# Masking the segment maxima of a graph attention kernel behind their transposition, with a mask that already lies in SBUF

## The chip, the cores and the metric

The kernel runs on one core of a Trainium2 chip. The metric is the device time of one execution in microseconds (us), taken as the median over several executions.

## What is computed

A graph attention layer with a feed-forward block is followed by a top-2 mixture of experts over 6250 nodes of 256 features. 100,000 edges, sorted by destination, carry attention of 8 heads. The part that matters here, cut from the reference:

```python
e = jax.nn.leaky_relu(a_src[src] + a_dst[dst], NEG_SLOPE)
emax = jax.ops.segment_max(e, dst, num_segments=N)
ee = jnp.exp(e - emax[dst])
denom = jax.ops.segment_sum(ee, dst, num_segments=N)
alpha = ee / denom[dst]
msg = h[src] * alpha[:, :, None]
agg = jax.ops.segment_sum(msg, dst, num_segments=N)
```

## The kernel before, in words

The program has four stages one behind another: nodes, edges, the layer's feed-forward block, experts. The change lies in the edge stage. It goes through the edges in 55 groups of 8 steps. A step is a block of 256 edges seen from one window of 128 destination nodes. 16 indirect gathers on GpSimd fetch the source rows of a group (L762), up to four groups ahead.

Every engine runs a loop written by hand over g = -1 to 55, which works in one turn on three groups: n = g + 1 (its maxima), g (its scores and messages) and g - 1 (its sums). The engines run their own instructions in the order in which they are written and meet through counting semaphores. In one turn, from the scan of group n on:

1. VectorE scans a_src along the edges with segment restarts (`tensor_tensor_scan`, L1053), so that the last edge of each segment holds the segment's maximum. It then multiplies by a row mask that is 1 at those last edges (L1055). The mask is `seg_last`, [64, 256], which SyncE loads per group from the scratch tensor `step_last` (L797).
2. TensorE turns the result, [64, 256] to [128, 2 x 64], into `b_cand` (L925).
3. ScalarE and VectorE split the values into three bf16 parts: high part (L876, ScalarE), rest (L1075, VectorE), middle part (L886, ScalarE), low part (L1080, VectorE). 16 products with one-hot matrices (L937, TensorE) then pick each node's maximum. VectorE reads that at the start of the next turn (L967).
4. In between VectorE computes the scores of group g (L1061, L1067, L1069, L1071). ScalarE takes the exponential (L883) and VectorE multiplies the gathered rows by it: `messages(g, 0)` to `messages(g, 2)`, three instructions on L1016. Four small ones (also L1016) follow in the next turn.
5. Behind L886 ScalarE widens the one-hot matrices of group g to f32 (L891, semaphore `oh_wide`). Without them TensorE cannot start the sums of group g.
6. Behind L937 TensorE does the sums of group g: eight steps of L948 for k = 0 to 7, two f32 matmuls a step, with a product for the residual (L828, L829) between k = 1 and k = 2 in 49 of the 55 turns. A f32 matmul has two records in the trace, so a step has four. VectorE adds each step's sum to its window (L1042), in the order of k.

The same mask lies in SBUF in another layout as well, `last_col`, [128, steps, 2], made once in the node stage. ScalarE copies its columns into the candidates (L873).

Of the kernel before, what the change touches and what calls it, by code (L numbers as in the profile page):

```python
# [10 lines left out]
ALU = mybir.AluOpType  # L11
# [3 lines left out]
P = 128  # L15
# [5 lines left out]
def build(nc, x, src, dst, gW, att_src, att_dst, g_bias, gW_res, ln1_g, ln1_b, ln2_g, ln2_b,  # L21
          f_w1, f_b1, f_w2, f_b2, Wr, br, ln_g, ln_b, W1, b1, W2, b2, out):
    N, D = x.shape
    HEADS, HD = att_src.shape
# [6 lines left out]
    EB = 256  # L31
    NEB = dst.shape[0] // EB
    WIN = NT + 1
    GS = 8
    NG = -(-(NEB + NT - 1) // GS)
    NSTEP = NG * GS
    NK = -(-NSTEP // P)
# [15 lines left out]
    with ctx:  # L53
        pe, dve, act, pool, sp = nc.tensor, nc.vector, nc.scalar, nc.gpsimd, nc.sync
# [4 lines left out]
        def dram(name, shape, dt=F32):  # L59
            return nc.dram_tensor(name, shape, dt, kind="Internal").ap()  # L60
# [17 lines left out]
        residual = dram("residual", [NT * P, D])  # L78
        turned = dram("turned", [NT, P, D])
        step_new = dram("step_new", [NK * P, EB])  # L80
        step_last = dram("step_last", [NK * P, EB])
        step_place = dram("step_place", [NK * P, EB], BF16)
        expert_rows = dram("expert_rows", [E * CAP + SLOT, XROW])
        WSZ = KC * HID
# [33 lines left out]
        def sb1(name, shape, dt=F32):  # L118
            return early.enter_context(nc.sbuf_tensor(name, shape, dt))
# [57 lines left out]
        iota_i = part(OT0 + 2 * GT * P - P, P).bitcast(I32)  # L177

        seg_new = [sb1(f"seg_new{i}", [HEADS * GS, EB]) for i in range(2)]
        seg_last = [sb1(f"seg_last{i}", [HEADS * GS, EB]) for i in range(2)]  # L180
        seg_max = sb1("seg_max", [HEADS * GS, EB])
        asrc = sb1("asrc", [P, 2, GS, HEADS])
        cand = sb1("cand", [P, 2, GS, 3, HEADS + 1], BF16)
# [371 lines left out]
        def prep_sp(i):  # L555
            if i == 0:
                with nc.allow_non_contiguous_dma(reason="one element per edge block"):
                    sp.dma_start(first[0:1, :], dst_rows[:, 0:1].rearrange("b o -> o b")).then_inc(prep_loaded, 16)
            if i == 6:
                sp.wait_ge(new_ready, 1)  # L560
                sp.dma_start(step_new.rearrange("(c p) e -> p c e", p=P), rows_n).then_inc(steps_stored, 16)
                sp.wait_ge(places_made, 1)
                sp.dma_start(step_place.rearrange("(c p) e -> p c e", p=P), rows_p).then_inc(place_rows_stored, 16)
            if i == 9:
                sp.wait_ge(last_ready, 1)
                sp.dma_start(step_last.rearrange("(c p) e -> p c e", p=P), rows_n).then_inc(steps_stored, 16)

        def prep_pool(i):
            if i == 0:
# [196 lines left out]
        def edges_sp():  # L766
            sp.dma_start(br_b[:, :], br.unsqueeze(0).to_broadcast([P, E])).then_inc(small_loaded, 16)
            for k in range(KC):
                sp.dma_start(wr_sb[:, k, :], Wr[k * P:(k + 1) * P, :]).then_inc(small_loaded, 16)
            with nc.allow_non_contiguous_dma(reason="small vectors, one element per partition"):  # L770
                sp.dma_start(g2[:, 0, :], ln2_g.rearrange("(k p) -> p k", p=P)).then_inc(small_loaded, 16)
                sp.dma_start(g2[:, 1, :], ln2_b.rearrange("(k p) -> p k", p=P)).then_inc(small_loaded, 16)
                sp.dma_start(fb1[:, :], f_b1.rearrange("(m p) -> p m", p=P)).then_inc(small_loaded, 16)
                for e in range(E):
                    sp.dma_start(epar[:, e, 0:KC], ln_g[e, :].rearrange("(k p) -> p k", p=P)).then_inc(small_loaded, 16)
                    sp.dma_start(epar[:, e, KC:2 * KC], ln_b[e, :].rearrange("(k p) -> p k", p=P)).then_inc(small_loaded, 16)
                    sp.dma_start(epar[:, e, 2 * KC:], b1[e, :].rearrange("(m p) -> p m", p=P)).then_inc(small_loaded, 16)
            for k in range(KC):
                sp.dma_start(Wres[:, k, :], gW_res[k * P:(k + 1) * P, :]).then_inc(res_consts, 16)
            sp.dma_start(bias_row[:, :], g_bias.unsqueeze(0)).then_inc(res_consts, 16)  # L780
            turned_all(sp)
            load_xn(0)
            load_xn(1)
            sp.wait_ge(steps_stored, 32)
            sp.wait_ge(place_rows_stored, 16)
            load_piece(0)
            load_piece(1)
            for g in range(NG):
                for i in pieces_of(g - 1):
                    store_piece(i)  # L790
                    if i + 2 < N_PIECES:
                        load_piece(i + 2)
                if g >= 2:
                    sp.wait_ge(masked, g - 1)
                r = slice(g * GS, (g + 1) * GS)
                sp.dma_start(seg_new[g % 2][:, :], step_new[r, :].unsqueeze(1).to_broadcast([GS, HEADS, EB])).then_inc(seg_loaded[g % 2], 16)
                sp.dma_start(seg_last[g % 2][:, :], step_last[r, :].unsqueeze(1).to_broadcast([GS, HEADS, EB])).then_inc(seg_loaded[g % 2], 16)  # L797
                if g >= 2:
                    sp.wait_ge(edge_vals, g - 1)
                sp.dma_start(onehot_t[g % 2].rearrange("p t n -> p (t n)"),  # L800
                             step_place[r, :].rearrange("k e -> (k e)").unsqueeze(0).to_broadcast([P, GS * EB])).then_inc(places_loaded[g % 2], 16)
                next_residual(g - 2)
            next_residual(NG - 2)
            next_residual(NG - 1)
# [32 lines left out]
        def edges_act():  # L837
            act.wait_ge(cols_copied, 2 * 3)
            act.wait_ge(new_ready, 1)
            act.wait_ge(steps_stored, 32)  # L840
            act.wait_ge(place_rows_stored, 16)
            for g in range(-1, NG + 1):
                n = g + 1
# [23 lines left out]
                if 0 <= g - 1 < NT:  # L867
                    keep_residual(g - 1)
                if n < NG:
                    values = b_cand[:, EB:EB + P].rearrange("p (j k h) -> p j k h", j=2, k=GS)  # L870
                    if n >= 1:
                        act.wait_ge(maxima_made, n)
                    act.copy(cand[:, :, :, 0, HEADS:HEADS + 1],  # L873
                             last_col[:, n * GS:(n + 1) * GS, :].rearrange("p k j -> p j k").unsqueeze(3))
                    act.wait_ge(cand_turned, n + 1)
                    act.copy(cand[:, :, :, 0, 0:HEADS], values).then_inc(cand_high, 1)  # L876
                if 0 <= g < NG:
                    act.wait_ge(scale_taken, g + 1)
                    act.wait_ge(scored, g + 1)
# [13 lines left out]
        def edges_pe():  # L893
# [5 lines left out]
            for g in range(-1, NG + 1):  # L899
# [20 lines left out]
                                        start=True, stop=True)  # L920
                    ins.then_inc(edge_vals, 1)
                if n < NG:
                    pe.wait_ge(masked, n + 1)
                    for j in range(2):
                        ins = pe.transpose(b_cand[:, EB + j * 64:EB + (j + 1) * 64], seg_max[:, j * P:(j + 1) * P], ident[0:64, 0:64])  # L925
                    ins.then_inc(cand_turned, 1)
# [25 lines left out]
        def edges_dve():  # L952
# [58 lines left out]
            def messages(g, m):  # L1011
                first_, end = PIECES_M[m]
                r = slice(first_, end)
                rows_ = gath[g % NGB][:, r, 0:AGG].rearrange("p t (h c) -> p t h c", c=HC)
                dve.wait_ge(weights_ready, g + 1)
                dve.tensor_tensor(rows_, rows_, wgt[:, r, :].unsqueeze(3).to_broadcast([P, end - first_, HEADS, HC]), ALU.mult).then_inc(weighted, 1)  # L1016

            dve.memset(cand[:, :, :, 1:3, HEADS:HEADS + 1], 0.0).then_inc(edge_setup, 1)
            dve.wait_ge(table_written, n_table)
            dve.wait_ge(steps_stored, 32)  # L1020
            dve.wait_ge(dve_step, dve_steps[0])
            for g in range(-1, NG + 1):
                n = g + 1
# [22 lines left out]
                if n < NG:  # L1046
                    for i in pieces_of(n):
                        low_piece(i)
                    dve.wait_ge(asrc_turned, n + 1)
                    dve.wait_ge(seg_loaded[n % 2], 32 * (n // 2 + 1))  # L1050
                    if n >= 1:
                        dve.wait_ge(cand_turned, n)
                    dve.tensor_tensor_scan(seg_max[:, :], seg_new[n % 2][:, :], b_asrc[0:HEADS * GS, 0:EB], -BIG, ALU.add, ALU.max).then_inc(scanned, 1)  # L1053
                    dve.wait_ge(scanned, n + 1)
                    dve.tensor_tensor(seg_max[:, :], seg_max[:, :], seg_last[n % 2][:, :], ALU.mult).then_inc(masked, 1)  # L1055
                if 0 <= g < NG:
                    gb = gath[g % NGB]
                    ev = edge_sum[:, :, :]
# [12 lines left out]
                    dve.tensor_tensor(score[:, :, :], score[:, :, :], ev[:, :, HEADS:16], ALU.subtract).then_inc(scored, 1)  # L1071
                if n < NG:
                    values = b_cand[:, EB:EB + P].rearrange("p (j k h) -> p j k h", j=2, k=GS)
                    dve.wait_ge(cand_high, n + 1)
                    dve.tensor_tensor(cand_rest[:, :, :, :], values, cand[:, :, :, 0, 0:HEADS], ALU.subtract).then_inc(cand_left, 1)  # L1075
                if 0 <= g < NG:
                    messages(g, 0)
                if n < NG:
                    dve.wait_ge(cand_middle, n + 1)
                    dve.tensor_tensor(cand[:, :, :, 2, 0:HEADS], cand_rest[:, :, :, :], cand[:, :, :, 1, 0:HEADS], ALU.subtract).then_inc(cand_split, 1)  # L1080
                if 0 <= g < NG:
                    messages(g, 1)
                    messages(g, 2)


# [875 lines left out]
```

## Time and profile before

| what | value |
|---|---|
| median of 3 runs | 2339.06 us (2338.97 to 2340.69) |
| profiled execution, its time | 2340.55 us |
| its span | 2339.3 us |
| edge stage, first to last scan | 134.3 to 1243.4 us, 55 scans |

The span is the profiled part of the execution, so 1.25 us lie around it. The edge stage holds nearly half of it. In the rows below a time is in us from the start of the span. A row of the timeline gives the start, the duration, the engine, the line, the operation, the tiles with their shape, how many instructions are merged in it, and in brackets the idle time of the engine before it with what ended it. The next instruction of an engine may start a little before the previous one's end as listed.

### The profile page before, as it was taken

To read this page: it belongs to the slowest core of one execution; us is meant where nothing else is said; L and a number is where in the kernel's file an instruction comes from. 1 tells how busy PE (TensorE), PEld (TensorE's weight loads), DVE (VectorE), ACT (ScalarE), POOL (GpSimd) and SP (SyncE) were. 2 spreads that over 40 slices of the span, in tenths; PEclk is the share of its full clock that TensorE was granted. 3 is DMA by queue.
4 is the path that set the end of the run, shared out by engine and by line. 5 is a ranking of instruction groups with operands and counts; after the bars stand their busy time and mean duration, and the time that the engine had idled before them with its cause. 6 is when DMAs were issued, how large, how long until landed. Compare 5 with 4: busy or idle time off the path is not lost.

```text
span 2339.3 us, 42815 instructions
## 1 busy us (share of the span) xinstructions
PE 1769.7 (76%) x12098; PEld 1544.0 (66%) x12098; DVE 1761.5 (75%) x5421; ACT 1554.6 (66%) x3225; POOL 1189.2 (51%) x1167
## 2 busy tenths in 40 slices
PE   5526666666666666666655899999299999999998
PEld 4414444444544444444444788888299999999998
DVE  7359999999999999999998788887355555555554
ACT  3366776777766667766663687886266666666665
POOL 3377777777777777777760134435122222222223
PEclk9857777777777777777777899999599999999999
DMA  7767777676777667777663223322835346435432
GB/s 229 198 182 211 212 212 209 197 208 206 211 225 205 200 203 205 219 211 200 198 175 113 73 90 97 96 77 81 237 44 120 50 110 155 95 47 153 85 47 37
DMA packets 276606, 358.06 MB, mean 153 GB/s; under 512 B 118917, under 2 KB 208862, under 8 KB 271634
## 3 DMA queue, kind: packets, MB, share of 16 engines
q1 hardware_dynamic: 211954, 202.64, 28.2%
q0 software_dynamic: 63840, 151.61, 27.2%
q8 instruction: 98, 1.61, 0.3%
q10 hardware_dynamic: 576, 1.09, 0.2%
q14 instruction: 138, 1.13, 0.2%
HBM read 460.74 MB, written 95.79 MB: 238 GB/s over the span
## 4 chain that ended last, share of the span: by engine, by line
PE 46%; DVE 32%; issue 12%; POOL 3%; DVEq 3%; ACT 3%; DMA 2%; SPq 0%; ACTq 0%; POOLq 0%
PE bank L1143 12%; PE bank L1144 12%; PE bank L1145 12%; PE bank L948 6%; DVE edge_mem L1016 5%; DVE win_mem L1042 3%; DVE edge_sum L1061 2%; POOL edge_mem L762 2%; DVE win_mem L1038 2%; DVE win_mem L980 2%; DVEq L977 2%; DVE piece_lo L1139 1%; DVE old L977 1%; DVE seg_max L1053 1%; DVE layer_rounded L1139 1%
## 5 line engine op out<-in xcount | busy, mean ns | idle before, releaser
L762 POOL DMA_INDIRECT edge_mem<-node_table,src_col x880 | 845.7, 961 | 281.8 <-issue 255.5
L1143 PE MATMUL bank<-expert_rounded 128*128 128x256 f32 x1792 | 509.1, 284 | 36.4 <-DVE expert_rounded L1139 30.8
L948 PE MATMUL bank<-edge_mem 128*128 128x264 f32 x1760 | 528.6, 458 | 10.2 <-DVE win_mem L1042 5.0
L1144 PE MATMUL bank<-expert_rounded 128*128 128x256 f32 x1792 | 508.7, 284 | 0.0
L1145 PE MATMUL bank<-expert_rounded 128*128 128x256 f32 x1792 | 508.6, 284 | 0.0
L948 PEld LDWEIGHTS bank<-edge_mem 128*128 128x128 f32 x1760 | 379.1, 225 | 125.1 <-issue 44.7
L1865 POOL DMA_INDIRECT out<-expert_mem,slot_tok x112 | 174.1, 1555 | 508.6 <-DVE expert_mem L1802 488.6
L1143 PEld LDWEIGHTS bank<-expert_rounded 128*128 128x128 f32 x1792 | 345.8, 193 | 36.6 <-issue 36.6
L1852 ACT ACTIVATE expert_mem<-bank,par 128x256 f32<-128x256 f32 x448 | 224.2, 500 | 200.9 <-PE bank L1145 200.9
L1139 DVE TENSOR_TENSOR expert_rounded<-expert_mem,expert_rounded 128x512 fp32r<-128x512 f32 x280 | 194.0, 693 | 215.3 <-ACT expert_rounded L1852 142.2
L1144 PEld LDWEIGHTS bank<-expert_rounded 128*128 128x128 f32 x1792 | 345.8, 193 | 0.0
L1145 PEld LDWEIGHTS bank<-expert_rounded 128*128 128x128 f32 x1792 | 345.7, 193 | 0.0
L1016 DVE TENSOR_TENSOR edge_mem<-edge_mem,bank 128x1056 f32<-128x1056 f32 x385 | 294.4, 777 | 13.8 <-ACT bank L883 13.8
L856 ACT ACTIVATE edge_mem<-iota,dst_col 128x128 bf16<-128x128 bf16 x880 | 262.9, 388 | 0.0
L1852 ACT ACTIVATE expert_rounded<-bank,par 128x256 fp32r<-128x256 f32 x448 | 225.0, 502 | 0.0
L1038 DVE TENSOR_TENSOR win_mem<-win_mem,bank 128x264 f32 x440 | 188.1, 427 | 17.2 <-issue 4.7
L1042 DVE TENSOR_TENSOR win_mem<-win_mem,bank 128x264 f32 x440 | 187.7, 427 | 4.0 <-PE bank L948 3.0
L937 PE MATMUL bank<-cand,edge_mem 128*128 128x27 bf16 x880 | 32.3, 186 | 185.3 <-DVE cand L1080 185.3
L876 ACT CAST cand<-bank 128x128 bf16<-128x128 f32 x55 | 16.1, 292 | 229.1 <-PE bank L925 229.0
L919 PE MATMUL bank<-parts,edge_mem 128*128 128x48 bf16 x880 | 41.5, 207 | 163.8 <-DVE parts L1009 163.8
L937 PEld LDWEIGHTS bank<-cand,edge_mem 128*128 128x128 bf16 x880 | 28.1, 104 | 193.8 <-issue 193.8
L919 PEld LDWEIGHTS bank<-parts,edge_mem 128*128 128x128 bf16 x880 | 34.6, 111 | 178.7 <-DVE parts L1009 178.7
(235 smaller groups left out, 3769.4 us busy)
## 6 DMA issues: line engine op xcount, KB each, us to landing
expert_rounded<-split_w SPq DMA_DIRECT2D x224, 1024.0 KB
edge_mem<-step_place SPq DMA_DIRECT2D x55, 512.0 KB, 7.2
split_w<-piece_hi SPq DMA_DIRECT2D x72, 256.0 KB
split_w<-piece_lo SPq DMA_DIRECT2D x72, 256.0 KB
piece_full<-in_L_ffn_W SPq DMA_DIRECT2D x64, 256.0 KB
expert_mem<-expert_rows SPq DMA_DIRECT2D x224, 64.0 KB, 2.8
edge_mem<-node_table,src_col POOLq DMA_INDIRECT x880
node_table<-win_mem SPq DMA_DIRECT2D x12, 544.0 KB, 4.3
```

The lines of the kernel that those rows point to most:

```text
L762: pool.indirect_dma_start(gath[g % NGB][:, t, :], None, node_table, bass.IndirectOffsetOnAxis(ap=src_col[:, k, t % 2:t % 2 + 1], axis=0)). ...
L856: ins = act.activation(o16[:, t, :], iota16[:, :], ACT.Abs, scale=-1.0, bias=dst_col[:, k, t % 2:t % 2 + 1])
L948: ins = pe.matmul(bank[4 + at % 3][:, 0:AGG], onehot[g % 2][:, 2 * k + j, :], gath[g % NGB][:, 2 * k + j, 0:AGG], start=(j == 0), stop=(j ...
L1016: dve.tensor_tensor(rows_, rows_, wgt[:, r, :].unsqueeze(3).to_broadcast([P, end - first_, HEADS, HC]), ALU.mult).then_inc(weighted, 1)
L1038: t_scaled = step(dve.tensor_tensor(acc_h, acc_h, scale[:, k, :].unsqueeze(2).to_broadcast([P, HEADS, HC]), ALU.mult))
L1042: dve.tensor_tensor(acc, acc, bank[4 + at % 3][:, 0:AGG], ALU.add).then_inc(added, 1)
L1139: return eng.tensor_tensor(lo, full, hi.bitcast(F32), ALU.subtract)
L1143: pe.matmul(out_ap, s_hi, m_lo, start=start, stop=False)
L1144: pe.matmul(out_ap, s_lo, m_hi, start=False, stop=False)
L1145: return pe.matmul(out_ap, s_hi, m_hi, start=False, stop=stop)
L1852: ins = act.activation(d, bank[1 + m % 4][:, 0:SLOT], ACT.Gelu, bias=par[jf % 3][:, 2 * KC + m:2 * KC + m + 1])
L1865: pool.indirect_dma_start(out, bass.IndirectOffsetOnAxis(ap=slot_tok[:, js % NTB, t:t + 1], axis=0), yout[js % 3][:, t, :], None, compute_ ...
```

## The change

The mask by `seg_last` right behind the scan (L1055) goes, and with it `seg_last`, its load (L797) and the store of `step_last` in the node stage. TensorE transposes the unmasked scan. VectorE masks the transposed values with `last_col` into a new SBUF tile `ended`, at the place where it computed the rest before. The high part on ScalarE now copies `ended` and so waits for the mask. The rest is computed behind message 0 where it stood ahead of it, the low part behind message 1 where it stood behind message 0.

```diff
@@ SyncE, node stage (i == 9) @@
-                sp.wait_ge(last_ready, 1)
-                sp.dma_start(step_last.rearrange("(c p) e -> p c e", p=P), rows_n).then_inc(steps_stored, 16)
@@ SyncE, each group @@
-                    sp.wait_ge(masked, g - 1)
+                    sp.wait_ge(scanned, g - 1)
                 sp.dma_start(seg_new[g % 2][:, :], step_new[r, :]...
-                sp.dma_start(seg_last[g % 2][:, :], step_last[r, :].unsqueeze(1).to_broadcast([GS, HEADS, EB])).then_inc(seg_loaded[g % 2], 16)
@@ ScalarE @@
-                    act.wait_ge(cand_turned, n + 1)
-                    act.copy(cand[:, :, :, 0, 0:HEADS], values).then_inc(cand_high, 1)
+                    act.wait_ge(masked, n + 1)
+                    act.copy(cand[:, :, :, 0, 0:HEADS], ended[:, :, :, :]).then_inc(cand_high, 1)
@@ TensorE @@
-                    pe.wait_ge(masked, n + 1)
+                    pe.wait_ge(scanned, n + 1)
+                    if n >= 1:
+                        pe.wait_ge(masked, n)
@@ VectorE @@
-                    dve.wait_ge(scanned, n + 1)
-                    dve.tensor_tensor(seg_max[:, :], seg_max[:, :], seg_last[n % 2][:, :], ALU.mult).then_inc(masked, 1)
...
-                    dve.wait_ge(cand_high, n + 1)
-                    dve.tensor_tensor(cand_rest[:, :, :, :], values, cand[:, :, :, 0, 0:HEADS], ALU.subtract).then_inc(cand_left, 1)
+                    dve.wait_ge(cand_turned, n + 1)
+                    dve.tensor_tensor(ended[:, :, :, :], values, last_col[:, n * GS:(n + 1) * GS, :].rearrange("p k j -> p j k").unsqueeze(3).to_broadcast([P, 2, GS, HEADS]),
+                                      ALU.mult).then_inc(masked, 1)
                 if 0 <= g < NG:
                     messages(g, 0)
+                if n < NG:
+                    dve.wait_ge(cand_high, n + 1)
+                    dve.tensor_tensor(cand_rest[:, :, :, :], ended[:, :, :, :], cand[:, :, :, 0, 0:HEADS], ALU.subtract).then_inc(cand_left, 1)
+                if 0 <= g < NG:
+                    messages(g, 1)
                 if n < NG:
                     dve.wait_ge(cand_middle, n + 1)
                     dve.tensor_tensor(cand[:, :, :, 2, 0:HEADS], cand_rest[:, :, :, :], cand[:, :, :, 1, 0:HEADS], ALU.subtract).then_inc(cand_split, 1)
                 if 0 <= g < NG:
-                    messages(g, 1)
                     messages(g, 2)
```

The order of instructions on VectorE from the scan to the next turn's first reduction, before, with the semaphores that each waits for:

```order
L1053 SCALAR_TENSOR_TENSOR seg_max<-seg_new,bank 64x256 [waits cand_turned,seg_loaded0,asrc_turned]
L1055 TENSOR_TENSOR seg_max<-seg_max,seg_last 64x256 [waits scanned]
L1061 TENSOR_REDUCE edge_sum<-bank 128x160 [waits edge_vals]
L1061 TENSOR_REDUCE edge_sum<-bank 128x96
L1071 TENSOR_TENSOR exponent<-exponent,edge_sum 128x128 [waits dve_step]
L1075 TENSOR_TENSOR cand_rest<-bank,cand 128x128 [waits cand_high]
L1016 TENSOR_TENSOR edge_mem<-edge_mem,bank 128x4x264 [waits weights_ready]
L1080 TENSOR_TENSOR cand<-cand_rest,cand 128x16x8 [waits cand_middle]
L1016 TENSOR_TENSOR edge_mem<-edge_mem,bank 128x4x264 [waits weights_ready] x2
L967 TENSOR_REDUCE max_sum<-bank 128x72 [waits maxima_made]
```

The same place after the change (line numbers of the changed kernel, in which L1012 is the message, L1069 the mask, L1075 the rest, L1080 the low part and L963 the reduction):

```order
L1049 SCALAR_TENSOR_TENSOR seg_max<-seg_new,bank 64x256 [waits cand_turned,seg_loaded0,asrc_turned]
L1055 TENSOR_REDUCE edge_sum<-bank 128x160 [waits edge_vals]
L1055 TENSOR_REDUCE edge_sum<-bank 128x96
L1065 TENSOR_TENSOR exponent<-exponent,edge_sum 128x128 [waits dve_step]
L1069 TENSOR_TENSOR ended<-bank,last_col 128x128 [waits cand_turned]
L1012 TENSOR_TENSOR edge_mem<-edge_mem,bank 128x4x264 [waits weights_ready]
L1075 TENSOR_TENSOR cand_rest<-ended,cand 128x128 [waits cand_high]
L1012 TENSOR_TENSOR edge_mem<-edge_mem,bank 128x4x264 [waits weights_ready]
L1080 TENSOR_TENSOR cand<-cand_rest,cand 128x16x8 [waits cand_middle]
L1012 TENSOR_TENSOR edge_mem<-edge_mem,bank 128x4x264 [waits weights_ready]
```

One instruction behind the scan is gone, one stands in the old place of the rest, and the rest and the low part each stand one message further back. On ScalarE at the same place, before:

```order
L876 CAST cand<-bank 128x16x8 [waits cand_turned]
L883 ACTIVATE bank<-exponent 128x192 [waits weighted,added,scored,scale_taken]
L886 CAST cand<-cand_rest 128x16x8 [waits cand_left]
L891 CAST edge_mem<-edge_mem 128x2048 [waits summed,oh_ready]
L849 COPY asrc<-edge_mem 128x128 [waits asrc_turned,gathered2]
```

And after, where L870 is the high part, L877 the exponential, L880 the middle part and L885 the widening:

```order
L870 CAST cand<-ended 128x16x8 [waits masked]
L877 ACTIVATE bank<-exponent 128x192 [waits weighted,added,scored,scale_taken]
L880 CAST cand<-cand_rest 128x16x8 [waits cand_left]
L885 CAST edge_mem<-edge_mem 128x2048 [waits summed,oh_ready]
L844 COPY asrc<-edge_mem 128x128 [waits asrc_turned,gathered2]
```

ScalarE's order is the same; what the high part waits for has changed from `cand_turned` (TensorE) to `masked` (VectorE).

## Rows read from the trace of the kernel before

**Rows 1.** The page: busy time of each engine, with share of the span.

```profile
PE 1769.7 (76%) x12098; PEld 1544.0 (66%) x12098; DVE 1761.5 (75%) x5421; ACT 1554.6 (66%) x3225; POOL 1189.2 (51%) x1167
```

**Rows 2.** Busy time of the engines in a stretch of the edge stage.

```profile
core 0: us, PE busy (x) PEld busy (x) DVE busy (x) ACT busy (x) POOL busy (x), PEclk, DMA share, GB/s
300.00:1200.00 900.00, 571.62 (x3228) 427.38 (x3228) 849.63 (x2775) 635.93 (x1201) 680.30 (x709) 0.75 0.72 208
```

**Rows 3.** VectorE's waits, 300 to 1250 us: total, times, longest.

```profile
DVE edge_mem L1016 <- ACT bank L883: 11.7, 47, 0.3
...
DVE win_mem L1042 <- PE bank L948: 1.9, 4, 0.8
```

**Rows 4.** The scan over the whole program: duration, first and last start.

```profile
L1053 DVE TENSOR_TENSOR_SCAN seg_max<-seg_new,bank x55: 669/672/673, 134.3 to 1243.4; 64x256 f32<-64x256 f32 x55
```

**Rows 5.** Timeline of VectorE in one turn, from its scan on.

```profile
812.48 0.67 DVE L1053 TENSOR_TENSOR_SCAN seg_max<-seg_new,bank 64x256 f32<-64x256 f32 x1
813.18 0.42 DVE L1055 TENSOR_TENSOR seg_max<-seg_max,seg_last 64x256 f32<-64x256 f32 x1
813.53 1.00 DVE L1061 TENSOR_REDUCE edge_sum<-bank 128x160 f32<-128x480 f32 x2
...
815.22 0.29 DVE L1071 TENSOR_TENSOR exponent<-exponent,edge_sum 128x128 f32<-128x128 f32 x1
815.42 0.28 DVE L1075 TENSOR_TENSOR cand_rest<-bank,cand 128x128 f32<-128x128 f32 x1
815.96 1.25 DVE L1016 TENSOR_TENSOR edge_mem<-edge_mem,bank 128x1056 f32<-128x1056 f32 x1 [0.25 <-ACT bank L883]
817.13 0.29 DVE L1080 TENSOR_TENSOR cand<-cand_rest,cand 128x128 bf16<-128x128 f32 x1
817.33 2.41 DVE L1016 TENSOR_TENSOR edge_mem<-edge_mem,bank 128x1056 f32<-128x1056 f32 x2
819.66 0.38 DVE L967 TENSOR_REDUCE max_sum<-bank 128x72 f32<-128x216 f32 x1
```

**Rows 6.** Timeline of ScalarE in the same turn.

```profile
814.17 0.29 ACT L876 CAST cand<-bank 128x128 bf16<-128x128 f32 x1 [5.10 <-PE bank L925]
815.59 0.33 ACT L883 ACTIVATE bank<-exponent 128x192 f32<-128x192 f32 x1 [1.13 <-DVE exponent L1071]
815.86 0.30 ACT L886 CAST cand<-cand_rest 128x128 bf16<-128x128 f32 x1
816.05 1.89 ACT L891 CAST edge_mem<-edge_mem 128x2048 f32<-128x2048 bf16 x1
```

**Rows 7.** Timeline of TensorE in the same turn.

```profile
817.52 0.59 PE L937 MATMUL bank<-cand,edge_mem 128*128 128x27 bf16 x16 [3.39 <-DVE cand L1080]
818.04 3.44 PE L948 MATMUL bank<-edge_mem 128*128 128x264 f32 x8
821.32 1.03 PE L828 MATMUL bank<-Wres,xn_in 128*128 128x256 f32 x4
...
822.90 1.16 PE L948 MATMUL bank<-edge_mem 128*128 128x264 f32 x4
```

**Rows 8.** Timeline of VectorE, same turn: it adds the sum of k = 2.

```profile
824.72 0.43 DVE L1042 TENSOR_TENSOR win_mem<-win_mem,bank 128x264 f32 x1
```

**Rows 9.** Timeline of TensorE in another turn, whose scan starts at 1038.25.

```profile
1043.29 0.59 PE L937 MATMUL bank<-cand,edge_mem 128*128 128x27 bf16 x16 [3.39 <-DVE cand L1080]
1043.81 3.86 PE L948 MATMUL bank<-edge_mem 128*128 128x264 f32 x8
1047.46 1.91 PE L828 MATMUL bank<-Wres,xn_in 128*128 128x256 f32 x4
...
1050.07 1.16 PE L948 MATMUL bank<-edge_mem 128*128 128x264 f32 x4
```

**Rows 10.** Timeline of VectorE in that turn: it adds the sum of k = 2.

```profile
1051.33 0.43 DVE L1042 TENSOR_TENSOR win_mem<-win_mem,bank 128x264 f32 x1 [0.77 <-PE bank L948]
```

**Rows 11.** Windows in the two turns; the granted clock is the third number from the end.

```profile
817.52:820.92 3.40, 3.40 (x23) 2.77 (x24) 3.10 (x7) 3.40 (x12) 2.49 (x4) 0.50 1.06 352
820.92:828.86 7.94, 7.87 (x33) 5.62 (x32) 7.29 (x32) 7.91 (x11) 6.11 (x7) 1.00 0.66 197
1043.29:1049.62 6.33, 6.33 (x29) 4.66 (x30) 6.00 (x19) 6.30 (x19) 4.80 (x6) 0.50 0.99 326
```

**Rows 12.** GpSimd's gathers in the stretch of rows 2, by line.

```profile
L762 POOL DMA_INDIRECT edge_mem<-node_table,src_col x709 | 680.8, 960 | 220.0 <-issue 204.3 <-PE bank L948 15.7
```

More of the change, by code:

```diff
@@ L80, in build @@
         step_new = dram("step_new", [NK * P, EB])
-        step_last = dram("step_last", [NK * P, EB])
         step_place = dram("step_place", [NK * P, EB], BF16)
@@ L179, in build @@
         seg_new = [sb1(f"seg_new{i}", [HEADS * GS, EB]) for i in range(2)]
-        seg_last = [sb1(f"seg_last{i}", [HEADS * GS, EB]) for i in range(2)]
+        ended = sb1("ended", [P, 2, GS, HEADS])
         seg_max = sb1("seg_max", [HEADS * GS, EB])
@@ L563, in prep_sp @@
                 sp.dma_start(step_place.rearrange("(c p) e -> p c e", p=P), rows_p).then_inc(place_rows_stored, 16)
-            if i == 9:
-                sp.wait_ge(last_ready, 1)
-                sp.dma_start(step_last.rearrange("(c p) e -> p c e", p=P), rows_n).then_inc(steps_stored, 16)
         def prep_pool(i):
@@ L783, in edges_sp @@
             load_xn(1)
-            sp.wait_ge(steps_stored, 32)
+            sp.wait_ge(steps_stored, 16)
             sp.wait_ge(place_rows_stored, 16)
@@ L839, in edges_act @@
             act.wait_ge(new_ready, 1)
-            act.wait_ge(steps_stored, 32)
+            act.wait_ge(steps_stored, 16)
             act.wait_ge(place_rows_stored, 16)
@@ L869, in edges_act @@
                 if n < NG:
-                    values = b_cand[:, EB:EB + P].rearrange("p (j k h) -> p j k h", j=2, k=GS)
                     if n >= 1:
@@ L1019, in edges_dve @@
             dve.wait_ge(table_written, n_table)
-            dve.wait_ge(steps_stored, 32)
+            dve.wait_ge(steps_stored, 16)
             dve.wait_ge(dve_step, dve_steps[0])
@@ L1049, in edges_dve @@
                     dve.wait_ge(asrc_turned, n + 1)
-                    dve.wait_ge(seg_loaded[n % 2], 32 * (n // 2 + 1))
+                    dve.wait_ge(seg_loaded[n % 2], 16 * (n // 2 + 1))
                     if n >= 1:
```

## The prediction

> **What bounds the kernel now.** I read the page first: over the whole span no engine is full, TensorE and VectorE stand at 76 and 75% [rows 1]. So the question is put to the stage. In the edge stage VectorE is busy 849.6 of 900 us, 94%, where TensorE has 64, ScalarE 71 and GpSimd 76% [rows 2]. VectorE's list of waits says how tight it is: of 950 us it loses 11.7 to the exponential of ScalarE, 0.25 in each of 47 turns, and only 1.9, in four turns, to TensorE's sums [rows 3]. A turn lasts (1243.4 - 134.3) / 54 = 20.54 us [rows 4]. So the turn is VectorE's program plus 0.25 for the exponential, and TensorE is just in time. An edit counts here by what it does to VectorE's sequence and by how much it delays what VectorE will wait for next.
>
> I count a turn from the start of its scan (812.48). Before [rows 5 to 7]: reductions at 1.05, L1071 at 2.74 to 3.03, rest at 2.94 to 3.22, exponential at 3.11 to 3.44, message 0 at 3.48, low part at 4.65, L967 at 7.18; on ScalarE the middle part at 3.38 and the widening of the one-hots at 3.57 to 5.46; on TensorE the candidates' products at 5.04, the sums at 5.56. TensorE starts its sums as soon as both its candidates' products and the widening are through; the two end together.
>
> **The mask behind the scan.** Gone. The scan takes 0.67, and an instruction that waits for nothing starts 0.07 ahead of its predecessor's end, as the reductions do behind the mask (813.60 against 813.53). So the reductions start at 0.60 instead of 1.05: minus 0.45 us a turn.
>
> **The new mask.** Nothing in the trace multiplies by a broadcast column of this layout. The nearest row is the rest itself, same shape, one operand in PSUM: 0.28 [rows 5]. It takes the rest's place, at 2.94 - 0.45 = 2.49, and ends at 2.77. From below 0.20 (the step from L1071 to L1075), from above 0.42 (the old mask); I take 0.28. The transposition is no issue: it has been through for more than a microsecond.
>
> **The exponential.** It stands behind the high part in ScalarE's queue. Before, the high part ran at 814.17, 1.4 us ahead, in idle time [rows 6]. Now it waits for the mask. It starts at 2.77 + 0.08 (L1071's end to L883: 815.51 to 815.59) = 2.85, and the exponential, 0.2 behind it (L886 to L891 is 0.19, L883 to L886 0.27), at 3.07, where its own scores would have let it start at 2.66. It ends at 3.40 and message 0 starts at 3.44 to 3.50; I take 3.47. Before it was 3.48. So the whole 0.45 is spent: VectorE stands idle from 2.77 to 3.47, 0.70 us, where it stood 0.25. A rule of the Trainium skill speaks against the change here too ("VectorE: DVE Perf Modes", section on the TRN2 errata): ScalarE's fixed cost is 224 cycles with its source in SBUF and 172 in PSUM, and the high part's source moves from PSUM to SBUF on a path that now counts. By the rule that would be an estimated 43 ns a turn, 2.4 us in all. The rows give 0.30 for the cast from SBUF (L886) and 0.29 for that from PSUM (L876) [rows 6], so about 0.01, or 0.5 us; I keep to the rows.
>
> **The rest.** Before, it filled the time in which VectorE waited for the exponential; the mask fills it now, and the rest stands behind message 0 with nothing to wait for. It adds the step of such an instruction, 0.20 (L1080 at 817.13 to the message at 817.33 [rows 5]). L967 comes at 3.47 + 1.17 + 0.20 + 1.17 + 0.20 + 1.17 = 7.38, against 7.18: plus 0.20 us a turn. The candidates' products are ready for it: low part at 6.01, products from 6.40 to 6.99 (before 0.39 behind the low part, for 0.59 [rows 7]).
>
> **What becomes late.** Every turn's sums stand behind these products and behind the widening. The products end at 6.99. The rest ends at 3.47 + 1.17 + 0.28 = 4.92; the middle part follows 0.08 later, the widening 0.19 behind it, at 5.19, and ends at 7.08. So the sums start at about 7.12 instead of 5.56, 1.56 later, while VectorE's own program is 0.20 later. VectorE adds k = 2 at 12.24 [rows 8], which would be 12.44. How long TensorE needs from its first sum to k = 2 depends on its clock: it resumes at half clock, 1.2 GHz, and gets 2.4 GHz after 3.4 us in this turn, after 6.3 us in the other [rows 11]. In the first, k = 2 is ready at 822.90 + 1.16 = 824.06, 6.02 behind the start at 818.04 [rows 7]; in the second 7.42 behind it [rows 9], and VectorE, taking it 0.10 later, has already waited 0.77 [rows 10]. After the change that makes 7.12 + 6.12 = 13.24 or 7.12 + 7.52 = 14.64, against 12.44: a wait of 0.8 to 2.2 us in each of the 49 turns with a residual product. I count no second wait behind k = 2, since by then the clock is at full in both turns. Which end holds? Before, only four turns of 47 had a wait of L1042 for the sums at all [rows 3], so a turn of 20.5 us met the early rise nearly always. A turn that is over a microsecond longer will not keep its place to the clock, so I expect turns of both kinds; I take 1.2, nearer to the early one, which the trace shows far more often.
>
> **Hidden.** The dropped load takes 0.6 to 1.3 us of SyncE's queue a group, but the scan of before never waits for it (no wait on it in the list of rows 3). GpSimd's 16 gathers take 16 x 1.26 = 20.1 us a turn (680.8 + 204.3 us for 709 [rows 12]), under any turn forecast here; but they would cap a gain at about 0.45 us a turn. ScalarE's program moves 1.6 us back and has 5.10 us idle ahead of L876 [rows 6].
>
> **Sum.** 49 turns x (0.20 + 1.2 - 0.1) + 5 x 0.20 = 65 us, where 0.1 stands for small waits of before that fall inside the new one. Against its own execution: 2340.55 + 65 = 2405.6; the median of the runs lies 1.5 lower, so 2404. A measurement of this kernel tells about 0.2%, 4.7 us, from no change.
>
> **The rivals.** (a) My forecast, a wait at k = 2 of 0.8 to 1.7 us: 49 x 0.9 to 49 x 1.8, 2383 to 2427. Chance 0.60.
> (b) TensorE's clock rises where it did, as counted from the scan (820.92, 8.44), though the sums start later. Then the 1.56 us of work that moves from half clock to full takes half the time: k = 2 is ready at 11.58 + 0.78, is taken 0.10 later, at 12.46, and there is no wait; with the rise one microsecond later it would be 12.96 and 0.5. The time is 49 x 0.2 to 49 x 0.7 more: 2349 to 2373. The rise of the first turn came 3.4 us behind TensorE's resumption, which speaks against it. The Trainium skill ("TensorE: Matmul & The Clock Gate", "What's actually happening") calls the throttled state the default, released by activity; by that, too, a later start means a later rise, and (a). Chance 0.20.
> (c) Every turn is like the second one: 49 x (0.20 + 2.2) = 118 us, 2457. For it speaks nothing but that such turns occur; against it the four of 47. Chance 0.09.
> (d) Faster. The place is ScalarE's queue between the high part and the exponential. If the exponential were held by less than 0.24 us behind its scores (I work out 0.41), L967 would come earlier than the 7.18 of before; if it were not held at all, message 0 would start at 3.03 and VectorE would gain 0.25 a turn. The sums would then begin at 6.68, with k = 2 at 12.8 against 11.99, so it pays only if the clock also rises as early as in (b): 54 x -0.25 = -13 us, 2326. GpSimd's 20.1 us bound it at -24, 2315. Chance 0.05.
> (e) No difference: the two effects cancel, or VectorE's other small stalls swallow 0.20. 2335 to 2344. Chance 0.06.
>
> **Range and chances.** (a), (b) and what lies between them hold 0.8: 2353 to 2430. Slower by over 0.2% 0.89, within 0.06, faster 0.05.
>
> **What would show it.** In the profile after: reductions 0.60 behind the scan (the first term); the wait of the first message for the exponential about 0.7 us in place of 0.25 (the second); L967 at 7.4 (the third); the sums' first matmul at 7.1, released by ScalarE's widening (the fourth); and a wait of VectorE's L1042 for TensorE once a turn, near 1.2 us on the mean and varying with the clock (the fifth and largest). The prediction fails if the sums start early, if the clock's rise doesn't move with them, or if the wait at k = 2 isn't there.

## The result

The changed kernel takes 2408.38 us (median of 4 runs, 2406.47 to 2410.94), the kernel before 2339.01 us in the same comparison: a ratio of 1.0297 (95% interval 1.0285 to 1.031), 69 us slower. The profiled execution has a span of 2405.2 us.

Busy time in the windows of the edge stage (first to last scan) and of what follows it, of the changed kernel:

```profile
core 0: us, PE busy (x) PEld busy (x) DVE busy (x) ACT busy (x) POOL busy (x), PEclk, DMA share, GB/s
134.10:1311.90 1177.80, 686.73 (x3918) 521.11 (x3918) 1029.30 (x3393) 776.92 (x1470) 809.76 (x853) 0.73 0.64 190
1311.90:2405.20 1093.30, 1008.76 (x7850) 973.47 (x7850) 658.63 (x1798) 724.41 (x1610) 320.68 (x253) 0.96 0.39 94
```

And of the kernel before:

```profile
134.30:1243.40 1109.10, 690.57 (x3918) 514.00 (x3918) 1035.83 (x3392) 779.04 (x1470) 818.60 (x852) 0.75 0.70 204
1243.40:2339.30 1095.90, 1010.64 (x7850) 974.27 (x7850) 658.86 (x1798) 724.50 (x1610) 320.66 (x253) 0.96 0.39 94
```

The scan runs from 134.3 to 1243.4 us before [rows 4] and from 134.1 to 1311.9 us now: 1177.8 us instead of 1109.1, or 21.81 us a turn instead of 20.54. The stage is 68.7 us longer and what follows it 2.6 us shorter, so all of the loss lies in the edge stage. VectorE is busy there for less time than before (1029.30 against 1035.83 us), and the stage is longer: what grew is its idle time.

VectorE's waits in the changed kernel, 300 to 1300 us (total, times, longest). The kernel before had 1.9 us for the sums and 11.7 us for the exponential between 300 and 1250 us, also some 46 turns [rows 3]:

```profile
DVE win_mem L1038 <- PE bank L944: 51.9, 42, 2.1
DVE edge_mem L1012 <- ACT bank L877: 28.0, 46, 0.6
```

L1038 adds a step's sum to the window (L1042 before), L1012 is a message. There are now 42 waits for the sums instead of four, 1.24 us each. Over the whole program they come to 61.0 us in 50 waits, against 3.0 us in seven before. The wait for the exponential is 0.61 us a turn instead of 0.25.

One turn of the changed kernel on VectorE, whose scan starts at 966.86 (timeline):

```profile
966.86 0.67 DVE L1049 TENSOR_TENSOR_SCAN seg_max<-seg_new,bank 64x256 f32<-64x256 f32 x1
967.46 0.99 DVE L1055 TENSOR_REDUCE edge_sum<-bank 128x160 f32<-128x480 f32 x2
...
969.13 0.29 DVE L1065 TENSOR_TENSOR exponent<-exponent,edge_sum 128x128 f32<-128x128 f32 x1
969.34 0.28 DVE L1069 TENSOR_TENSOR ended<-bank,last_col 128x128 f32<-128x128 f32 x1
970.24 1.25 DVE L1012 TENSOR_TENSOR edge_mem<-edge_mem,bank 128x1056 f32<-128x1056 f32 x1 [0.61 <-ACT bank L877]
971.41 0.28 DVE L1075 TENSOR_TENSOR cand_rest<-ended,cand 128x128 f32<-128x128 f32 x1
...
974.14 0.37 DVE L963 TENSOR_REDUCE max_sum<-bank 128x72 f32<-128x216 f32 x1
...
979.85 0.43 DVE L1038 TENSOR_TENSOR win_mem<-win_mem,bank 128x264 f32 x1 [0.68 <-PE bank L944]
```

The same turn on ScalarE and on TensorE:

```profile
969.66 0.32 ACT L870 CAST cand<-ended 128x128 bf16<-128x128 f32 x1 [5.61 <-DVE ended L1069]
969.87 0.34 ACT L877 ACTIVATE bank<-exponent 128x192 f32<-128x192 f32 x1
971.72 0.32 ACT L880 CAST cand<-cand_rest 128x128 bf16<-128x128 f32 x1 [1.52 <-DVE cand_rest L1075]
971.93 1.89 ACT L885 CAST edge_mem<-edge_mem 128x2048 f32<-128x2048 bf16 x1
```

```profile
973.16 0.59 PE L933 MATMUL bank<-cand,edge_mem 128*128 128x27 bf16 x16 [5.10 <-DVE cand L1080]
973.92 3.24 PE L944 MATMUL bank<-edge_mem 128*128 128x264 f32 x8 [0.17 <-issue]
977.00 1.03 PE L823 MATMUL bank<-Wres,xn_in 128*128 128x256 f32 x4
...
978.58 1.16 PE L944 MATMUL bank<-edge_mem 128*128 128x264 f32 x4
```

The reader can follow the chain backwards. VectorE takes the sum of k = 2 at 979.85, 0.11 us after TensorE ends it at 979.74. TensorE began its sums at 973.92, 7.06 us behind the scan instead of 5.56 [rows 7], and 0.10 us after ScalarE had ended the widening of the one-hots (971.93 + 1.89 = 973.82). ScalarE began that right behind the middle part, for which it had stood idle 1.52 us. The middle part waited for the rest (L1075), which stands behind message 0. The candidates' products, which wait for the low part, ended at 973.75, only 0.07 us ahead of the widening. So either of the two moved parts alone might have held the sums nearly as long; no run moves one without the other.

The other kind of turn, on TensorE and VectorE, with its scan at 526.66:

```profile
533.72 3.86 PE L944 MATMUL bank<-edge_mem 128*128 128x264 f32 x8 [0.17 <-issue]
537.37 1.91 PE L823 MATMUL bank<-Wres,xn_in 128*128 128x256 f32 x4
...
539.96 1.16 PE L944 MATMUL bank<-edge_mem 128*128 128x264 f32 x4
```

```profile
541.23 0.43 DVE L1038 TENSOR_TENSOR win_mem<-win_mem,bank 128x264 f32 x1 [2.13 <-PE bank L944]
```

The windows go with the difference between 2.13 us here and 0.68 in the first. The third number from the end is TensorE's granted clock, at half in both stretches, for 3.2 us behind TensorE's resumption in the first turn and for 6.5 us in the second:

```profile
973.16:976.40 3.24, 3.07 (x22) 2.48 (x23) 2.94 (x10) 3.24 (x11) 2.33 (x4) 0.50 0.64 206
532.96:539.50 6.54, 6.37 (x29) 4.64 (x30) 5.68 (x21) 6.51 (x19) 5.01 (x6) 0.50 0.53 155
```

Two turns are a thin base, so here are all 42 turns with a residual product from 300 us on, read from the clock records of both traces. "Rise" is the time from the start of the candidates' products to the full clock; the wait is VectorE's for the sums, on the mean.

| rise | turns before, wait | turns after, wait |
|---|---|---|
| under 3.8 us | 8, 0.00 us | 8, 0.53 us |
| 3.8 to 5 us | 31, 0.01 us | 16, 0.92 us |
| over 5 us | 3, 0.55 us | 18, 1.80 us |

Two things grew: the wait at every rise, by what the later start of the sums takes from their margin, and the number of turns with a late rise, from 3 to 18. Why the late rises became more frequent is not shown.

### The profile page after: what moved, and what is told of

The parts are those of the page before. It is cut to its first block, busy times and chain, and to the rows that moved or that the text cites. A ratio compares the mean times of both kernels' runs of the same rounds, so it can differ in the third digit from the quotient of the medians.

```text
span 2405.2 us, 42813 instructions
## 1 busy us (share of the span) xinstructions
PE 1766.5 (73%) x12098; PEld 1551.9 (65%) x12098; DVE 1755.0 (73%) x5421; ACT 1552.3 (65%) x3225; POOL 1179.6 (49%) x1167
## 4 chain that ended last, share of the span: by engine, by line
PE 51%; DVE 28%; issue 10%; ACT 5%; POOL 2%; DMA 2%; DVEq 2%; SPq 0%; ACTq 0%; POOLq 0%
PE bank L1142 12%; PE bank L1144 11%; PE bank L1143 11%; PE bank L944 10%; DVE edge_mem L1012 5%; DVE win_mem L1038 3%; DVE edge_sum L1055 2%; PE bank L823 2%; DVE win_mem L1034 1%; DVE piece_lo L1138 1%; POOL edge_mem L758 1%; ACT edge_mem L851 1%; DVE layer_rounded L1138 1%; PE bank L824 1%; PE bank L933 1%
## 5 line engine op out<-in xcount | busy, mean ns | idle before, releaser
L758 POOL DMA_INDIRECT edge_mem<-node_table,src_col x880 | 836.1, 950 | 359.7 <-issue 250.9
L944 PE MATMUL bank<-edge_mem 128*128 128x264 f32 x1760 | 515.0, 455 | 13.8 <-issue 9.1
L944 PEld LDWEIGHTS bank<-edge_mem 128*128 128x128 f32 x1760 | 385.0, 226 | 113.3 <-issue 28.0
L1012 DVE TENSOR_TENSOR edge_mem<-edge_mem,bank 128x1056 f32<-128x1056 f32 x385 | 298.7, 776 | 33.4 <-ACT bank L877 33.4
L1038 DVE TENSOR_TENSOR win_mem<-win_mem,bank 128x264 f32 x440 | 187.5, 426 | 64.3 <-PE bank L944 61.0
L870 ACT CAST cand<-ended 128x128 bf16<-128x128 f32 x55 | 17.8, 323 | 307.0 <-DVE ended L1069 307.0
```

What stands on the lines that cost most here:

```text
L758: pool.indirect_dma_start(gath[g % NGB][:, t, :], None, node_table, bass.IndirectOffsetOnAxis(ap=src_col[:, k, t % 2:t % 2 + 1], axis=0)). ...
L944: ins = pe.matmul(bank[4 + at % 3][:, 0:AGG], onehot[g % 2][:, 2 * k + j, :], gath[g % NGB][:, 2 * k + j, 0:AGG], start=(j == 0), stop=(j ...
L1038: dve.tensor_tensor(acc, acc, bank[4 + at % 3][:, 0:AGG], ALU.add).then_inc(added, 1)
```

## The experiments

Twelve runs were made in three groups, two on a chip that I call A and one on chip B. There the kernel before itself takes 2606.08, 2577.66 (both A) and 2576.5 us (B), 10 to 11% more than in the first comparison, whose chip is not on record; I take it for a third. So every number below is compared with the kernel before in the same group. The changed kernel was run once more, in the last group on A. The ratios, each with its 95% interval, are estimates over the single executions; they differ from the quotients of the medians by up to 0.0013. What differs in these groups is told behind the experiments.

**The changed kernel again.**

> The changed kernel itself, as the reference for the experiments: the chips of the runs so far took 10 to 11% longer for the kernel before than the one of the first measurement. Theory A: 1.027 to 1.032 of before on a chip like the first; on one like the later ones the loss of the later split alone, 2.3%, and up to 3.5%.

2673.37 us against 2577.66: 1.038 (1.0364 to 1.0396), 96 us. It is slower there as well, by more than on the first chip and above the 3.5% that I gave as the most.

**The later split alone, in the kernel before.** Mask, its load and everything else stay. The edit moves two instructions of VectorE:

```diff
-                rest
                 messages(g, 0)
-                low part
+                rest
                 messages(g, 1)
+                low part
                 messages(g, 2)
```

> The kernel before with the later split alone (rest behind message 0, low part behind message 1; mask and its load as before). Theory A (the loss is the late start of the sums, which waits for the split on both ways): sums start 7.1 us behind the scan, L1042 waits 1.0 to 1.3 us a turn, time 2400 to 2415 like the change. Rival B (the loss comes from the mask that holds the exponential): only 0.2 us a turn, about 2350.

2669.73 us against 2606.08: 1.0235 (1.0203 to 1.0267), 63.7 us, as expected. In the last group, beside the changed kernel:

> The later split alone, once more beside the changed kernel. Theory A: the same time as the changed kernel within 0.5%. Rival B: less than half of its loss.

2660.17 us against 2577.66: 1.0325 (1.031 to 1.0341), 82.5 us of the changed kernel's 95.7, 86%. The two times differ by 0.5%, the most that theory A allowed. The waits of VectorE in the changed kernel and in this one, last group:

```profile
DVE edge_sum L1055 <- remote: 142.6, 38, 4.2
DVE win_mem L1038 <- PE bank L944: 42.3, 38, 2.0
DVE edge_mem L1012 <- ACT bank L877: 15.2, 25, 0.6
```

```profile
DVE edge_sum L1061 <- remote: 129.8, 39, 3.8
DVE win_mem L1042 <- PE bank L948: 47.7, 39, 2.1
DVE edge_mem L1016 <- ACT bank L883: 14.4, 32, 0.5
```

The wait for the sums is there without any change to the mask: 1.22 us against 1.11, and 1.24 on the first chip. Rival B is out as the main loss. The mask is not free beside the late split, though: the changed kernel takes 13.2 us more than this one, and no execution of the one (2672.26 us and more) is as fast as the slowest of the other (2662.04).

**The mask alone: the changed kernel with the split in its old places.**

```diff
+                rest
                 messages(g, 0)
-                rest
-                messages(g, 1)
                 low part
+                messages(g, 1)
                 messages(g, 2)
```

> The changed kernel with the split in its old places (mask, rest, message 0, low part, messages 1 and 2). Theory A: the sums start at 5.6 us behind the scan again, no wait at k = 2, and the 0.45 us of the old mask is spent on the held exponential: 2336 to 2343, no difference from before. Rival B: the held exponential and the mask keep most of the loss, above 2380.

2609.15 us against 2606.08: 1.0005 (0.9985 to 1.0024). With the split in its old places, the mask behind the transposition, with the dropped transfer and all its waits, makes no difference that can be told. The wait for the sums has shrunk:

```profile
DVE win_mem L1038 <- PE bank L944: 9.1, 17, 1.0
```

**The residual product later.** The changed kernel with the product for the residual behind k = 5:

```diff
-                        if k == 1 and g - 1 < NT:
+                        if k == 5 and g - 1 < NT:
                             residual_product(g - 1)
```

> The changed kernel with the residual product behind k = 5 instead of k = 1. Theory A (VectorE's wait at k = 2 is there because the residual product at half clock stands ahead of that sum): the wait goes, 0.2 us a turn is left, 2346 to 2356. Rival C (TensorE as a whole is late, so that the wait only moves to k = 3 or to k = 6): 2385 or more.

2622.54 us against 2606.08: 1.0057 (1.0039 to 1.0075). In the last group:

> The changed kernel with the residual product behind k = 5, once more beside it. Theory A: VectorE's wait at k = 2 goes, 45 us or more faster than the changed kernel, 5 to 17 us slower than before. Rival C: at least half of the loss stays.

2590.62 us against 2577.66: 1.0048 (1.0031 to 1.0065), 83 us faster than the changed kernel, 13 slower than before. TensorE starts its sums as late behind the reductions as in the changed kernel (both 6.5 us, medians). Only that product has left its place ahead of k = 2. These are VectorE's waits for TensorE's sums at L1038, last group, and the largest of its other waits:

```profile
DVE win_mem L1034 <- issue: 36.0, 50, 1.3
DVE old L973 <- issue: 34.2, 38, 1.9
DVE max_sum L963 <- remote: 26.8, 15, 2.5
...
DVE edge_sum L1055 <- remote: 9.9, 7, 2.0
...
DVE win_mem L1038 <- PE bank L944: 6.1, 9, 1.6
```

Against 42.3 us in 38 waits that ties the wait for the sums to the product's place ahead of k = 2, and it does not come back at a later step. It does not account for the whole gain. A turn is 1.6 us shorter on the mean (24.27 against 25.88 us), and the wait for the sums gives 0.9 of it. The other waits changed as well: the one ahead of the reductions, 142.6 us in the changed kernel, is down to 20.2 us (9.9 of it `remote`), and waits ahead of small instructions, for which the trace names no cause, stand in its place. What is left, 13 us, is not explained; the 0.10 us a turn by which L963 comes later on the first chip (7.28 behind the scan instead of 7.18) makes 5 us.

**The exponential first.** The changed kernel with ScalarE's exponential ahead of the high part.

```diff
-                    act.wait_ge(masked, n + 1)
-                    act.copy(cand[:, :, :, 0, 0:HEADS], ended[:, :, :, :]).then_inc(cand_high, 1)
                 if 0 <= g < NG:
                     ...
                     act.activation(b_exp, exponent[:, :, :], ACT.Exp).then_inc(weights_ready, 1)
+                if n < NG:
+                    act.wait_ge(masked, n + 1)
+                    act.copy(cand[:, :, :, 0, 0:HEADS], ended[:, :, :, :]).then_inc(cand_high, 1)
```

> The changed kernel with ScalarE's exponential ahead of the high part in its queue, so that message 0 waits for the scores only. Theory A: the exponential's hold of 0.4 us a turn goes, the sums start 0.4 us earlier, and VectorE's wait at k = 2 changes little, since both sides move: 0.4 us a turn or about 22 us faster than the changed kernel, still about 45 us slower than before. Rival B (the hold is the main loss): 50 us or more faster than the changed kernel.

1.0319 (1.0298 to 1.034). One of the four executions took 9335.51 us and is left out here; the median of the other three is 2655.25 us, against 2576.5. The changed kernel was not run in this group, but the run with the load kept, below, was: 2673.83 us, 18.6 us more than this one. Against the changed kernel's loss in the last group, 95.7 us, this one's 78.8 is 17 us less. 22 us was expected, and rival B wanted 50. From the reductions to message 0 it is 2.45 us instead of 2.81 (medians), so the hold is gone; the wait for the sums is not:

```profile
DVE win_mem L1039 <- PE bank L945: 48.6, 39, 2.1
```

**The load kept.** The changed kernel with the store of `step_last` and the load of `seg_last`, which nobody reads:

```diff
+                sp.dma_start(seg_last[g % 2][:, :], step_last[r, :].unsqueeze(1).to_broadcast([GS, HEADS, EB])).then_inc(seg_loaded[g % 2], 16)
```

> The changed kernel with the store of step_last and the load of seg_last as before, though nobody uses the mask (VectorE's scan waits for its landing as before). Theory A: the transfer was hidden, same time as the changed kernel within 0.2%. Rival F (the dropped transfer gave something back that the change's loss hides): 5 to 15 us slower than the changed kernel.

2673.83 us against the changed kernel's 2673.37, in another group on the other chip with nearly the same reference (2576.5 and 2577.66). No cost of the transfer shows, as far as two groups can be compared.

**TensorE kept at work.** Six products more on TensorE behind the transposition of the scan (excerpt; the waits for their tiles are left out):

```diff
+                    for j in range(6):
+                        pe.matmul(bank[3][:, D:2 * D], ident[:, :], Wres[:, j % KC, :], start=True, stop=True)
```

> The changed kernel with six f32 products of 128x256 more per turn on TensorE, behind the transposition of the scan, whose result nobody reads; they only keep TensorE at work in the gap ahead of the candidates' products. Theory A (the sums before k = 2 are late because they run at half clock): the clock is full when the sums start, k = 2 is ready at about 7.1 + 4.8 = 11.9 behind the scan, VectorE's wait there goes, and a turn is 1.0 to 1.3 us shorter than the changed kernel's: 45 to 65 us faster than it. Rival E (the clock has no part, the start alone counts): no gain or a loss against the changed kernel.

2679.29 us against 2576.5: 1.0397 (1.038 to 1.0415), no gain. But it does not test what it was meant to. The windows behind the first added product, of the gap and of the first sums, in one turn:

```profile
816.54:822.17 5.63, 5.49 (x13) 3.87 (x12) 2.11 (x7) 0.54 (x2) 2.88 (x4) 0.50 1.04 354
822.17:825.58 3.41, 0.49 (x16) 0.48 (x16) 3.41 (x5) 1.93 (x2) 1.96 (x2) 1.00 0.76 248
825.85:829.00 3.15, 3.15 (x7) 2.48 (x8) 2.85 (x12) 3.15 (x12) 2.47 (x3) 0.50 0.30 81
```

The added products ran at half clock, the full clock came when they were through, held while TensorE stood nearly idle, and was gone again when the sums began. The gap between the transposition and the candidates' products is longer on these chips than on the first, and the first turn of the stage takes 61.6 us here where the other runs of these groups take 48.3 to 48.5. The run is inconclusive on the clock.

**The mask earlier.** The changed kernel with the mask between the two reductions and the scores, and the split in its old places. The high part then falls into ScalarE's idle time and holds nothing (excerpt of the edit).

```diff
+                    if n < NG:
+                        mask(n)
                     dve.wait_ge(dve_step, t)
```

> The changed kernel with the mask between the two reductions and the scores, and the split in its old places. The high part then runs in ScalarE's idle time again and holds nothing. Theory A: VectorE gains 0.45 and pays 0.1 to 0.2 for the mask, 0.25 to 0.35 us a turn: 2320 to 2326. Rival D (something other than VectorE sets a turn near 20.5 us, so that a shorter program of VectorE gives nothing): 2334 to 2340.

2596.29 us against 2606.08: 0.9955 (0.9938 to 0.9972). Once more, in the last group:

> Mask between the reductions and the scores, split in its old places, once more. Theory A: faster than before, by 14 to 20 us on a chip like the first, by about 10 us (0.4%) on one like the later ones. Rival D: within 0.2% of before.

2576.11 us against 2577.66: 0.9998 (0.9989 to 1.0008). So the gain did not repeat. VectorE's program is shorter as worked out, which the timeline of one turn of the last run shows:

```profile
806.01 0.67 DVE L1055 TENSOR_TENSOR_SCAN seg_max<-seg_new,bank 64x256 f32<-64x256 f32 x1
809.96 1.02 DVE L1061 TENSOR_REDUCE edge_sum<-bank 128x160 f32<-128x480 f32 x2 [3.28 <-remote]
810.90 0.28 DVE L1017 TENSOR_TENSOR ended<-bank,last_col 128x128 f32<-128x128 f32 x1
...
812.48 1.25 DVE L1012 TENSOR_TENSOR edge_mem<-edge_mem,bank 128x1056 f32<-128x1056 f32 x1 [0.25 <-ACT bank L877]
...
816.18 0.38 DVE L963 TENSOR_REDUCE max_sum<-bank 128x72 f32<-128x216 f32 x1
```

The mask takes 0.20 of the line. From the reductions to L963 it is 6.22 us against 6.13 in the kernel before [rows 5], and the reductions could start 0.45 earlier: 0.36 us a turn. But VectorE stands idle for 3.28 us ahead of the reductions here, and a wait that long can swallow it. Whether the early mask would gain on the first chip, where that wait is absent, no run shows.

**Both.** The earlier mask with the residual product behind k = 5.

> Mask between the reductions and the scores, split in its old places, and the residual product behind k = 5. Theory A: as with the early mask alone, 0.25 to 0.35 us a turn faster than before, plus the few waits of k = 2 for the sums (0.04 us a turn): 14 to 20 us faster than before. Rival D (GpSimd's 20.1 us a turn or the sums cap it): no more than 5 us.

2588.8 us against 2576.5: 1.0051 (1.0035 to 1.0068), slower, where a gain was expected. Its waits of L1044 for the sums are small (4.3 us in six); its idle time stands ahead of small instructions of VectorE, as `issue`, in which the engine waits for nothing that the trace shows:

```profile
DVE win_mem L1040 <- issue: 59.6, 65, 1.8
DVE old L973 <- issue: 54.1, 75, 2.0
```

Moving the residual product is no improvement there.

**What differs on these chips.** In nearly every turn of the runs with the residual product in its old place, with either order of the split, VectorE waits up to 4.3 us ahead of the reductions, for the semaphore of TensorE's edge values, though TensorE's own records of them end before. The trace names no releaser (`remote`). In the three runs with the residual product behind k = 5 it is at most 2.0 us, in 4 to 9 turns, and waits as `issue` stand elsewhere. The first turn of the stage takes 48.3 us or more instead of 19.4 (19.6 in the changed kernel), most of it ahead of single instructions with nothing that the trace shows them to wait for. Neither occurs in the first comparison. Every trace of these groups has such waits; none was taken there of the kernel before. I did not find their source. So the experiments price the change in turns that hold other idle time as well, and that the same shares hold on the first chip is argued from its own waits, not tested.

## Why the prediction was right

2404 us was forecast and 2408.4 measured, inside 2353 to 2430. By its steps:

- **The mask behind the scan.** Reductions 0.60 us behind the scan: 967.46 - 966.86. Right.
- **The new mask.** 0.28 us, as the row of the rest said.
- **The exponential.** Forecast idle 0.70, measured 0.61; message 0 at 3.37 to 3.38 behind the scan instead of 3.47. The exponential followed the high part by 0.21 and the high part its mask sooner than I had taken. Of the 0.45 us that the old mask gave back, 0.10 was left. The price of the high part I had wrong, if by little: L870 takes 0.32 us from SBUF, L876 took 0.29 from PSUM [rows 6]. The 0.03 us lie nearer to the estimate of 43 ns that I had worked out from the Trainium skill ("VectorE: DVE Perf Modes", section on the TRN2 errata) than to the 0.01 of my rows; for the duration the page was the better guide.
- **The rest.** 0.20 us behind message 0, as forecast. L963 comes at 7.28 instead of 7.38, for the 0.10 above: plus 0.10 us a turn, not 0.20.
- **What becomes late.** Sums forecast at 7.12, measured at 7.06, behind the widening. The wait at k = 2 was forecast between 0.8 and 2.2 us, 1.2 on the mean: 0.68 and 2.13 in the two turns shown, 1.24 on the mean over 42. The two ends were worked out and held. The mean was a choice between them, and how near it came is luck: over 49 turns the ends lie 69 us apart. One premise of it was wrong, too. The four waits of before did not show that nearly every turn met the early rise; only 8 of 42 turns did, and most had a rise in between, which the margin of before still covered. That both kinds of turn would come, and not the early rise alone, was argued from the turn's length only. The trace bears out that they came: the wait is the longer the later the clock rises. That the half clock is the cause of the spread is read from rows; the run meant to take it away did not.
- **The sum.** The waits for the sums grew by 61.0 - 3.0 = 58 us, and 0.10 us in each of 54 turns makes 5 more: 63 of the 68.7 us that the stage grew by. The other 5 or 6 us I cannot assign. I had 49 x (0.20 + 1.2 - 0.1) + 1 = 65, so the term of the rest was twice too large and the whole came out right in part because something else took its place.
- **Rivals.** (b), an unmoved clock, fell with the windows: the rise came 3.2 and 6.5 us behind TensorE's resumption; counted from the scan it came at 11.0 us on the mean of the 42 turns, 9.2 before. (c), every turn like the second, fell with the 24 of 42 turns whose rise was earlier, and (e), no difference, with the time. (d) would have needed the exponential to be held less. Its other half, the exponential first, was tried and is worth 17 to 19 us, far from enough alone. The transfer showed no cost. One sum of the prediction is off: the gathers take (680.8 + 204.3) / 709 = 1.25 us each, 20.0 a turn instead of 20.1, so they would cap a gain at 0.57 us a turn, 31 us in all. Only the bound of (d) used it.

The change has two parts that its words join. The mask behind the transposition costs nothing that can be told when the split stays in its old places, and 13 us beside the late split. The later split carries the loss: 86% of it in the last group. On the first chip the growth of the waits for the sums, which the late split brings on, makes 58 of 69 us; the split alone was not run there.

## What to carry to other kernels

An instruction that only fills the idle time of one engine may be the head of another engine's queue. Before it is moved back behind a long instruction, count what stands behind its consumer: here a cast of 0.3 us (the middle part) waits for the rest, the widening of the one-hots stands behind that cast, and the sums, which VectorE needs six microseconds later, stand behind the widening. Look then not at the first result that is late but at the first whose margin is smaller than the delay, and price that margin at both of TensorE's clocks. And work that nobody waits for soon, like the residual product here, should not stand ahead of such a result, which is worth testing by itself, since it moves other waits.

## What the runs showed of the hardware

The same program ran 10 to 11% slower in three later groups on two chips (2576.5 to 2606.08 us against 2339.01). For the changed kernel, of which there are traces of both, 233 of the 267 us lie in the edge stage, with waits that the trace cannot name. The chip is not all of it: on chip A the kernel before took 2606.08 us in one group and 2577.66 in another. A gain of 0.45% in one group was 0.02% in another on that same chip, and the loss of the later split was 2.35% and 3.25%. So differences under one per cent of this kernel are not safe across groups, whatever the interval of one says.

TensorE's granted clock was at half (0.50) whenever the candidates' products began, in both traces of the first comparison. In the turns with sums it rose to full 3.0 to 6.5 us later. With the late rise the same eight records of the sums took 3.86 us instead of 3.24, and the residual product 1.91 us instead of 1.03. In the turn shown of the run with six added products it rose behind them and had fallen again by the first sums, with 0.49 us of TensorE's work in the 3.41 us between.
